# Self-attention with a distance decay in a decoder layer: the diagonal's triangles cleared on GpSimd, zero rows in the operands, two operand buffers, the memory turned during the first maxima

## The chip, the core and the metric

The kernel runs on one core of one Trainium2 chip. The metric is the device time of one execution in microseconds (us), taken as the median of the runs. The engines named here are TensorE (PE; its weight loads are PEld), VectorE (DVE), ScalarE (ACT), GpSimd (POOL) and SyncE (SP), which issues most DMAs.

## What is computed

One decoder layer on x of 1024 tokens by 128 features, in three residual steps, each on a layer norm of x:

```
x = x + self_attention(norm(x))        # 16 heads of 8 features, no causal mask
x = x + cross_attention(norm(x), ctx, mask)   # one head, 6404 memory rows
x = x + ffn(norm(x))                   # weights and activations rounded to FP4 blocks of 16
```

The change lies in the self-attention and in what prepares the cross-attention:

```
latent = (k + v) @ W_down_kv;  k_rec = latent @ W_up_k;  v_rec = latent @ W_up_v
scores = einsum(qh, k_rec) / sqrt(128)
scores = scores * exp(-0.01 * abs(t_q - t_k))
out    = softmax(scores) @ v_rec @ W_o
```

The factor exp(-0.01 |t_q - t_k|) splits into a product of a query part and a key part, but with other signs above the diagonal than below it. So there are two pairs of operands, QL and KL ("lower") and QU and KU ("upper"). Each is split into three bf16 parts that together carry nine products, hence 72 rows of 8 features; three further rows carry the negative row maximum of each query against ones in the keys.

## The kernel before

Heads are taken in four groups g of four heads. For each group and each half of the queries (eight half groups hg) the kernel does two things, one half group or so apart.

**Maxima.** For 16 units (4 heads x 4 tiles of 128 queries) PE multiplies QL by all 1024 keys KL (`max_unit`: two matmuls of 512 columns, 72 rows deep) into one of two pairs of PSUM banks, and DVE multiplies by the decay table and takes the row maximum (`max_unit` on DVE, line 671). After 16 units PE turns the maxima (`max_rows`, line 930), DVE splits them in three bf16 parts (`shift_split`) and SP stores them into row 72 to 74 of the query operands (`load_shift`, line 304, six DMAs).

**Scores, exponentials, values.** 64 blocks gb of four units: a unit is one head, one tile of 128 keys and 512 queries. PE writes its transposed scores into one of three banks (`scores`), ACT takes the exponential into `probs` (line 537), PE multiplies with the values into bank 3 (`pv`, line 969, float32, four heads side by side in 32 columns each). Units 0 and 2 of each block hold the diagonal: their 128x128 diagonal tile is neither wholly lower nor wholly upper. PE computes it from QL and KL without the maximum (72 rows), DVE multiplies it in PSUM by `diagT` (line 747), and PE adds the negative maximum with a matmul of `ones_rows` (line 958). ACT waits for that.

PE's order is written out by hand: the token list `ORDER` in each block, with two maxima turns ("A" and "B") between scores. DVE's order follows it: diagonal product, one maxima turn, twice in a block. So the scores of a block wait for DVE's queue. Maxima run `MAX_LEAD` = 9 turns ahead of a half group.

Operands live in three buffers (`NB = 3`), so groups 0 to 2 are loaded early. Ctx (3.28 MB, called mem) is loaded when the scores of group 1 are done, turned on PE in blocks 53 to 59 (`mem_tiles`, line 981) and split into high and low parts on DVE (`mem_parts`, lines 692 and 694) once the maxima are over. The FFN weights' scales are DVE work in blocks 8 to 10 (`weight_scales`). When the self-attention's last values are done, SP begins to load the mask pieces (512 KB each, line 352) of the cross-attention into the room of `v_ext`; only the first piece is there before. GpSimd turns each piece into floats (line 430), DVE adds it to the logits (line 775).

Of the kernel before, what the change touches and what calls it, by code (L numbers as in the profile page):

```python
# [23 lines left out]
SHIFT_ROW = 72  # L24
MATH_ROWS = 72
# [5 lines left out]
def decoder_layer(nc, x, ctx, mask, w_q, w_k, w_v, w_o, w_down_kv, w_up_k, w_up_v,  # L31
# [27 lines left out]
    MAX_LEAD = 9  # L59
    MEM_BLOCK = (NG * NH * UNITS - UNITS - MAX_LEAD + 3) // 2  # L60
    EARLY_BLOCK = NG * NH * (S // P) - 3
    SCALE_BLOCK = NT
# [4 lines left out]
    with ExitStack() as stack:  # L67
# [8 lines left out]
        SLOTS = 2 * PARTS - 1  # L76

# [3 lines left out]

        ident = sb("ident", [P, P])
        wq_sb = sb("wq_sb", [P, D]); wk_sb = sb("wk_sb", [P, D]); wv_sb = sb("wv_sb", [P, D])
        wo_sb = sb("wo_sb", [P, D]); wdn_sb = sb("wdn_sb", [P, DL])
        wuk_sb = sb("wuk_sb", [DL, D]); wuv_sb = sb("wuv_sb", [DL, D])
        xw_sb = sb("xw_sb", [P, D]); xwT = sb("xwT", [P, D]); xb_sb = sb("xb_sb", [P, 1])
        half_neg = sb("half_neg", [P, NT])
        ones_rows = sb("ones_rows", [P, P], BF16)
# [11 lines left out]
        diagT = sb("diagT", [P, P])  # L100
# [6 lines left out]

        memT_lo = sb("memT_lo", [P, NK * P], F32R)
        qc = sb("qc", [P, 2, P])
# [5 lines left out]
        NB = 3  # L115
        OPW = HG * S
        with ExitStack() as self_stack:
            def sb1(name, shape, dt=F32):
                return self_stack.enter_context(nc.sbuf_tensor(name, shape, dt))
            ops = [sb1(f"operands_{b}", [P, 4, HG, S], BF16) for b in range(NB)]  # L120
            probs = sb1("probs", [P, 2 * HG, BANK])
# [8 lines left out]
        memT_hi = sb("memT_hi", [P, NK * P], F32R)  # L130
        fb = sb("fb", [P, 4, FF]); sb("pad_2", [P, OPB - NK * D - 4 * FF])
        logits_1 = sb("logits_1", [P, S2]); sb("pad_3", [P, 16 * BANK - S2])
# [20 lines left out]
        def early_turn(k):  # L153
            return (None, 1, 2, 4, 5, 6)[k] if 0 <= k < 6 else -1
# [18 lines left out]
        ones_src = xqT[:, 0:P // 2].bitcast(BF16)  # L173
        xT = ops[2][:, 2, 0:2, :].rearrange("p h n -> p (h n)").bitcast(F32)
# [7 lines left out]
        parts_sb = ops[1][:, 0:PARTS, :, :].rearrange("p w h n -> p (w h) n").rearrange("p (w a) n -> p w a n", w=4)  # L182
        iota_i = ops[2][:, 0, 0:4, :].rearrange("p h n -> p (h n)")[:, 0:2 * (2 * S - P)].bitcast(I32)
        iota_d = ops[2][:, 1, 0:4, :].rearrange("p h n -> p (h n)")[:, 0:2 * (2 * S - P)].bitcast(I32)
# [3 lines left out]
        s_tab = sem("tables_ready"); s_one = [sem(f"ones_loaded_{b}") for b in range(NB)]; s_pool = sem("pool_chain"); s_ones = sem("ones_rows_ready")  # L188
# [13 lines left out]
        s_dr = sem("diag_scores_ready"); s_dd = sem("diag_decayed")  # L202
        s_st = sem("scoresT_ready"); s_sd = sem("diag_scoresT_ready"); s_p = sem("probs_ready"); s_pv = sem("pv_block_done"); s_ot = sem("oT_taken")
# [3 lines left out]
        s_ql = sem("qc_low_ready"); s_mlo = sem("memT_low_ready"); s_mhi = sem("memT_high_ready"); s_dg = sem("diagT_ready")  # L207
# [43 lines left out]
        ROW_BANKS = (4, 5, 7)  # L251

# [8 lines left out]
        def _(sp):  # L261
# [18 lines left out]
            def load_ones(b):  # L280
                for w in (KL, KU):
                    sp.dma_start(ops[b][SHIFT_ROW:FULL_ROWS, w, :, :].rearrange("p h (a n) -> p (h a) n", n=P),
                                 ones_src[0:PARTS, :].unsqueeze(1).broadcast_to([PARTS, HG * S // P, P])).then_inc(s_one[b], 16)

            def load_operand(g, w):

# [10 lines left out]

            def load_shift(hg):
# [8 lines left out]
            sp.wait_ge(s_ones, 1)  # L307
            load_ones(0)
# [9 lines left out]
            load_ones(1)  # L318
            for w in range(4):
                load_operand(1, w)  # L320
            load_shift(1)
            sp.wait_ge(s_iota2, 1)
            sp.wait_ge(s_tab, 2)
            sp.wait_ge(s_v, 1)
            load_ones(2)
            for w in range(4):
                load_operand(2, w)
            load_shift(2)
            sp.wait_ge(s_st, 1 * 2 * BLKS)
            for w in range(4):  # L330
                load_operand(3, w)
            load_shift(3)
            load_shift(4)
            sp.wait_ge(s_st, 2 * 2 * BLKS)
            sp.dma_start(mem[:, 0:NKF, :], ctx[0, 0:NKF * P].rearrange("(t p) d -> p t d", p=P)).then_inc(s_mem, 16)
            sp.dma_start(mem[0:KREM, NKF, :], ctx[0, NKF * P:S2]).then_inc(s_mem, 16)
            for hg in range(5, NG * NH):
                load_shift(hg)
            sp.wait_ge(s_mxd, NG * NH * UNITS)
            sp.dma_start(mask_room(0, MP), mask[0, 0:P, 0:MP]).then_inc(s_mk0, 16)  # L340

            for t in range(NT + 1):
                for m in range(NMP if t < NT else 0):
# [3 lines left out]
                    if n == 1:  # L347
                        sp.wait_ge(s_pv, NG * BLKS)
# [12 lines left out]
        def _(pool):  # L361
            chain = [0]

            def link(ins):
# [12 lines left out]
            link(pool.memset(ones_src[:, :], 1.0))  # L377
            pool.affine_select(out=ones_rows[:, :], in_=ones_src[:, :], compare_op=ALU.is_ge, fill=0.0, base=-SHIFT_ROW,
                               pattern=[[0, P]], channel_multiplier=1).then_inc(s_ones, 1)
            pool.wait_ge(s_ones, 1)  # L380
# [9 lines left out]
            pool.wait_ge(s_iota2, 1)  # L390
            pool.wait_ge(s_dg, 1)
# [30 lines left out]

            def mask_piece(n):
# [10 lines left out]
            for n in range(NMP + 1 + LEAD // 2):  # L434
                if n == 1:
                    rstd_of(0, s_o6, s_o7)
# [18 lines left out]
        def _(act):  # L455
# [6 lines left out]

            act.wait_ge(s_wk, 16 * 5)
# [39 lines left out]
            act.wait_ge(s_mt, 1)  # L503
            act.activation(diagT[:, :], PS[:, 5, 0:P], ACT.Copy).then_inc(s_dg, 1)

            def take_oT(half):
                act.wait_ge(s_pv, NT * (half + 1))
# [21 lines left out]
            for g in range(NG):  # L529
                for b in range(BLKS):  # L530
                    gb = g * BLKS + b
                    for h in range(HG):
                        u = gb * HG + h
                        act.wait_ge(s_st if h % 2 else s_sd, 2 * gb + h // 2 + 1)
                        if gb >= 2 and h == 0:
                            act.wait_ge(s_pv, gb - 1)
                        act.activation(probs[:, (gb % 2) * HG + h, :], PS[:, u % 3, :], ACT.Exp).then_inc(s_p, 1)  # L537
                        if h % 2 == 1:
                            attn_step(0, early_turn(2 * (gb - EARLY_BLOCK) + h // 2))

                    if gb > 0 and gb % NT == 0:
                        take_oT(gb // NT - 1)
# [69 lines left out]
        def _(dve):  # L612
# [10 lines left out]

            dve.wait_ge(s_x, 16)
# [61 lines left out]
            def mem_parts(c):  # L686
                k0, kw = chunk(c)
                src = PS[:, 4 + c % 4, 0:kw]
                dve.wait_ge(s_mt, c + 2)
                if c == 0:  # L690
                    dve.wait_ge(s_st, 3 * 2 * BLKS)
# [174 lines left out]
        def _(pe):  # L866
# [186 lines left out]
            for gb in range(NG * BLKS):  # L1053
                u, mu = gb * HG, UNITS + MAX_LEAD + 2 * gb
                c = 2 * (gb - MEM_BLOCK)
                for tok in ORDER:
                    if tok == "s0": shift_diag(u)
# [145 lines left out]
```

## Time and profile before

| what | value |
|---|---|
| median of 3 runs (lowest to highest) | 581.99 us (580.92 to 586.65) |
| the profiled execution | 584.69 us, span 583.0 us, mean granted clock 0.893 |
| PE busy | 504.6 us, 87% |
| DVE busy | 403.5 us, 69% |
| ACT busy | 301.2 us, 52% |
| POOL busy | 102.3 us, 18% |
| chain of waits by engine | PE 66%, DVE 25%, issue 3%, DMA 2% |

Three stages share the span: preparation and first maxima to 65.6 us, the 64 blocks to 292.0 us, the cross-attention and FFN after that. The granted clock is the share of TensorE's full 2.4 GHz that was granted; 0.50 is 1.2 GHz. A busy share is an average over these stages, so it does not tell which engine holds up which stage.

### The profile page before, as it was taken

The page shows a single profiled execution, that of the slowest core. Times are in us where ns is not written, and L with a number is a line of the kernel's source. Part 1 is how long each engine was busy: PE and PEld are TensorE (multiplying, and loading weights), DVE is VectorE, ACT ScalarE, POOL GpSimd, SP SyncE. Part 2 cuts the span into 40 slices and gives each one's busy share as a digit, 9 for nine tenths or more (in the row PEclk, how much of TensorE's full clock was granted, in tenths as well). Part 3 has the DMA queues.
Part 4 walks back from the last instruction along what each step waited for, and adds up shares of the span by engine and source line. Part 5 has one row for each costly group of instructions (what it writes and reads, how often), then busy time and mean ns, then how long its engine had stood idle before and what let it go on. Part 6 is the DMA issues. An engine that isn't in the chain of part 4 may idle for free.

```text
span 583.0 us, 9028 instructions
## 1 busy us (share of the span) xinstructions
PE 504.6 (87%) x3222; PEld 321.0 (55%) x3222; DVE 403.5 (69%) x1026; ACT 301.2 (52%) x601; POOL 102.3 (18%) x119
## 2 busy tenths in 40 slices
PE   7258999889999999999887998989899898989953
PEld 6101233223233333345365997978789797878851
DVE  3889869879698988889377345756646566664443
ACT  4710256447475757677716572726446372638420
POOL 6020000980000000000034322221312212210000
PEclk9755579879698989899989998989989998999985
DMA  2690535307000800001057524323232422400000
GB/s 65 191 276 22 102 66 103 65 2 161 5 1 3 226 3 1 3 3 37 1 190 224 146 83 117 115 72 110 87 110 86 146 87 79 139 15 6 1 6 5
DMA packets 20727, 46.04 MB, mean 79 GB/s; under 512 B 4470, under 2 KB 9786, under 8 KB 20106
## 3 DMA queue, kind: packets, MB, share of 16 engines
q1 hardware_dynamic: 19930, 44.74, 27.9%
q8 instruction: 26, 0.43, 0.3%
q0 software_dynamic: 224, 0.54, 0.3%
q10 hardware_dynamic: 528, 0.18, 0.2%
q14 instruction: 19, 0.16, 0.1%
HBM read 40.39 MB, written 4.72 MB: 77 GB/s over the span
## 4 chain that ended last, share of the span: by engine, by line
PE 66%; DVE 25%; issue 3%; DMA 2%; ACT 2%; POOL 0%; SPq 0%; DVEq 0%; ACTq 0%; POOLq 0%
PE banks L868 43%; PE banks L969 11%; DVE banks L671 8%; PE banks L1101 6%; PE banks L958 3%; DVE logits L775 3%; DVE fa L811 1%; DMA operands<-query_parts 1%; DVE qc_lo L729 1%; PE banks L981 1%; DVE fa L810 1%; DVE fa L806 1%; DVE f_small L802 1%; ACT probs L537 1%; DMA x_sb<-in_x 1%
## 5 line engine op out<-in xcount | busy, mean ns | idle before, releaser
L537 ACT ACTIVATE probs<-banks 128x512 f32<-128x512 f32 x256 | 139.1, 596 | 117.4 <-PE banks L958 115.3
L868 PE MATMUL banks<-operands 72*128 72x512 bf16 (+5 forms) x704 | 158.3, 360 | 14.6 <-DMA operands<-query_parts 8.0
L671 DVE CUSTOM_DVE_ANT_0 banks<-banks,decay 128x1024 f32<-128x1024 f32 x128 | 156.5, 1228 | 15.1 <-PE banks L868 11.2
L868 PEld LDWEIGHTS banks<-mem,pT 128*128 128x128 f32 (+1 forms) x816 | 107.9, 195 | 7.7
L868 PE MATMUL banks<-mem,pT 128*128 128x128 f32 (+1 forms) x816 | 111.5, 279 | 0.0
L868 PEld LDWEIGHTS banks<-operands 72*128 72x128 bf16 (+1 forms) x704 | 62.0, 104 | 82.1 <-DVE row_max L671 24.5
L775 DVE CUSTOM_DVE_ANT_0 logits<-banks,mring 128x512 f32<-128x512 f32 (+1 forms) x102 | 67.4, 668 | 46.6 <-PE banks L868 23.2
L559 ACT ACTIVATE pT<-banks 128x512 f32<-128x512 f32 (+1 forms) x104 | 60.4, 581 | 52.6 <-PE banks L1101 52.6
L969 PE MATMUL banks<-probs,v_ext 128*32 128x512 f32 x512 | 76.6, 673 | 0.7 <-ACT probs L537 0.7
L430 POOL TENSOR_SCALAR mring<-mring 128x1024 f32<-128x1024 int32 (+1 forms) x55 | 52.7, 959 | 90.3 <-DMA mring<-in_mask_BxSxS_ik 88.1
L868 PE MATMUL banks<-memT_hi,qc_hi 128*128 128x512 f32 (+1 forms) x104 | 50.4, 485 | 17.7 <-DVE cmax L775 17.7
L1101 PE MATMUL banks<-ident,logits 128*128 128x128 f32 (+1 forms) x408 | 63.5, 279 | 0.0
L549 ACT ACTIVATE logits<-logits,neg_max 128x1024 f32<-128x1024 f32 (+1 forms) x56 | 58.8, 1051 | 6.4 <-DVE neg_max L782 6.4
L958 PEld LDWEIGHTS banks<-operands,ones_rows 75*128 75x128 bf16 x128 | 12.5, 98 | 83.8 <-DVE banks L747 67.9
L747 DVE TENSOR_TENSOR banks<-banks,diagT 128x128 f32<-128x128 f32 x128 | 40.6, 317 | 21.1 <-PE banks L868 21.0
L1101 PEld LDWEIGHTS banks<-ident,logits 128*128 128x128 f32 (+1 forms) x408 | 49.4, 143 | 4.0 <-issue 2.0
L868 PE MATMUL banks<-memT_hi,qc_lo 128*128 128x512 f32 (+1 forms) x104 | 41.4, 398 | 0.0
L868 PE MATMUL banks<-memT_lo,qc_hi 128*128 128x512 f32 (+1 forms) x104 | 41.1, 395 | 0.0
L958 PE MATMUL banks<-operands,ones_rows 75*128 75x128 bf16 x128 | 29.8, 233 | 12.5 <-DVE banks L747 12.3
L420 POOL TENSOR_TENSOR rstd<-mv,half_neg 128x1 f32<-128x1 f32 x16 | 8.8, 552 | 146.3 <-DVE mv L817 83.2
L868 PEld LDWEIGHTS banks<-memT_hi,qc_hi 128*128 128x128 f32 x104 | 20.7, 199 | 20.4 <-DVE cmax L775 19.7
L430 POOL TENSOR_SCALAR mask<-mask 128x1024 f32<-128x1024 int32 x1 | 1.0, 1046 | 135.5 <-DMA mask<-in_mask_BxSxS_ik 135.5
(162 smaller groups left out, 456.0 us busy)
## 6 DMA issues: line engine op xcount, KB each, us to landing
mring<-in_mask_BxSxS_ik SPq DMA_DIRECT2D x47, 512.0 KB, 3.5
operands<-key_parts SPq DMA_DIRECT2D x24, 192.0 KB
operands<-query_parts SPq DMA_DIRECT2D x24, 192.0 KB
key_parts<-operands SPq DMA_DIRECT2D x10, 256.0 KB, 3.5
query_parts<-operands SPq DMA_DIRECT2D x4, 384.0 KB, 4.7
mring<-in_mask_BxSxS_ik SPq DMA_DIRECT2D x8, 130.0 KB, 2.1
operands<-shift_parts SPq DMA_DIRECT2D x48, 4.0 KB, 1.7
x_sb<-in_x SPq DMA_DIRECT2D x1, 512.0 KB, 4.4
```

What stands on the lines that cost most here:

```text
L420: pool.tensor_tensor(rstd[:, t:t + 1], mv[:, t, 1:2], half_neg[:, t:t + 1], ALU.pow).then_inc(done, 1)
L430: pool.tensor_scalar(src.bitcast(F32), src, -1.0, -NEG, ALU.add, ALU.mult).then_inc(s_ma, 1)
L537: act.activation(probs[:, (gb % 2) * HG + h, :], PS[:, u % 3, :], ACT.Exp).then_inc(s_p, 1)
L549: act.activation(y, y, ACT.Exp, bias=neg_max[:, t:t + 1], accum_out=esum[:, t, e:e + 1]).then_inc(s_e, 1)
L559: last = act.activation(pT[:, n % 3, 0:o], PS[:, 2 + n % 2, 0:o], ACT.Copy)
L671: dve.tensor_tensor_reduce(out=rows, in0=rows, in1=decay[:, off:off + S], scale=1.0, scalar=-3.0e38, op0=ALU.mult, op1=ALU.max, accum_out= ...
L747: dve.tensor_tensor(PS[:, u % 3, c0:c0 + P], PS[:, u % 3, c0:c0 + P], diagT[:, :], ALU.mult).then_inc(s_dd, 1)
L775: dve.tensor_tensor_reduce(out=logits_sb(t)[:, k0:k0 + kw], in0=PS[:, logits_bank(n), 0:kw], in1=mk, scale=1.0, scalar=-3.0e38, op0=ALU.ad ...
L868: return pe.matmul(o, a, b, start=start, stop=stop)
L958: pe.matmul(PS[:, u % 3, d0:d0 + P], ones_rows[0:FULL_ROWS, :], queries(gb // BLKS % NB, QL, half)[0:FULL_ROWS, h, d0:d0 + P], start=False ...
L969: last = pe.matmul(PS[h * VW:(h + 1) * VW, 3, :], v_ext[:, kt, g * HG + h, :], probs[:, (gb % 2) * HG + i, :], start=(b % NT == 0), stop=( ...
L1101: last = pe.transpose(PS[0:kw, 2 + n % 2, j * P:(j + 1) * P], logits_sb(t)[:, k * P:k * P + kw], ident[:, :])
```

## The change

1. A block's diagonal units take their diagonal tile as if it were lower (with the maximum's rows). For every pair of blocks there is a ninth unit with the four heads' diagonal tiles computed as upper. ACT takes all nine exponentials; GpSimd then clears one triangle in each of the four lower tiles and the other triangle in the ninth unit (`affine_select`), and PE adds the ninth unit's values in `pv_diag`. `diagT`, `ones_rows`, the DVE product and the adding matmul are gone.
2. Forty rows of zeros stand between the 72 rows of parts and the three rows of the maximum, which move to row 112: maxima are 112 rows deep and scores 115 rows. The zeros come by DMA from a zeroed piece of `oT`, once for each buffer.
3. Two operand buffers instead of three. The decay table, the parts and the iotas lie elsewhere; the parts lie where the turned memory will be.
4. mem is loaded right behind the first group's lower operands, turned on PE in maxima turns 8 to 20 into banks 0 to 3, copied to its high part on ACT, reduced to its low part by a matmul with the negative identity on PE, and copied again on ACT. It lies in the room of operand buffer 1, so that buffer's constants and operands are loaded after it is turned, and mem is loaded a second time when the last scores are done.
5. `MAX_LEAD` is 7. The weights' scales stand ahead of the first maximum on DVE. `rstd` of tile 0 moves into the pairs on GpSimd.

```diff
-SHIFT_ROW = 72
-MATH_ROWS = 72
+PART_ROWS = 72
+MATH_ROWS = 112
+SHIFT_ROW = 112
...
-        NB = 3
+        NB = 2
...
+            def load_constants(b):
+                for w in range(4):
+                    sp.dma_start(ops[b][PART_ROWS:MATH_ROWS, w, :, :],
+                                 zero_rows.unsqueeze(1).broadcast_to([MATH_ROWS - PART_ROWS, HG, S])).then_inc(s_one[b], 16)
...
             load_operand(0, KL)
             load_operand(0, QL)
+            load_mem()
             store_parts(QU)
             store_parts(KU)
             load_operand(0, QU)
             load_operand(0, KU)
+            sp.wait_ge(s_mt, NC)
+            load_constants(1)
+            load_operand(1, KL)
+            load_operand(1, QL)
             load_shift(0)
...
             sp.wait_ge(s_mxd, NG * NH * UNITS)
             sp.dma_start(mask_room(0, MP), mask[0, 0:P, 0:MP]).then_inc(s_mk0, 16)
+            sp.wait_ge(s_st, PAIRS * PU)
+            load_mem()
...
+            for n in range(PAIRS):
+                d0 = 2 * n % NT // 2 * P
+                for j in (0, 2, 4, 6):
+                    diag = probs[:, j, d0:d0 + P]
+                    pool.wait_ge(s_p, n * PU + j + 1)
+                    pool.affine_select(out=diag, in_=diag, compare_op=ALU.is_ge, fill=0.0, base=0,
+                                       pattern=[[1, P]], channel_multiplier=-1).then_inc(s_sel, 1)
+                pool.wait_ge(s_p, (n + 1) * PU)
+                upper = probs[:, 2 * HG + n % 2, :].rearrange("p (h q) -> p h q", h=HG)
+                pool.affine_select(out=upper, in_=upper, compare_op=ALU.is_ge, fill=0.0, base=-1,
+                                   pattern=[[0, HG], [-1, P]], channel_multiplier=1).then_inc(s_sel, 1)
...
+            def mem_high(c):
+                act.wait_ge(s_mt, c + 1)
+                if c == 0:
+                    for w in range(4):
+                        act.wait_ge(s_scr[w], 16 * (SLOTS if w in (KL, KU) else NH))
+                act.activation(memT_hi[:, k0:k0 + kw], PS[:, c % 4, 0:kw], ACT.Copy).then_inc(s_mhi, 1)
...
+            def mem_rest(c):
+                pe.wait_ge(s_mhi, c + 1)
+                pe.matmul(PS[:, c % 4, 0:kw], ident_n, memT_hi[:, k0:k0 + kw], start=False, stop=True,
+                          skip_group_check=True).then_inc(s_mls, 1)
...
+            pe.wait_ge(s_mlo, NC)
+            for n in range(PAIRS):
+                mu, k = UNITS + MAX_LEAD + 4 * n, 4 * (n - EARLY_PAIR)
+                scores(n, 0)
+                max_turn(mu)
+                scores(n, 1)
+                if n > 0:
+                    pv(2 * n - 1)
+                scores(n, 2)
+                max_turn(mu + 1)
+                early(k)
+                scores(n, 3)
+                if n > 0:
+                    pv_diag(n - 1)
+                scores(n, 4)
+                max_turn(mu + 2)
+                early(k + 1)
+                scores(n, 5)
+                scores(n, 6)
+                pv(2 * n)
+                scores(n, 7)
+                max_turn(mu + 3)
+                early(k + 2)
+                scores(n, 8)
+                early(k + 3)
```

The order of SP's first loads before, from the stores of the lower parts on (a row is a DMA, with how often it is repeated):

```order
L277 DMA query_parts<-operands 128x3x512 x2
L296 DMA operands<-key_parts 24x4096 x3
L296 DMA operands<-query_parts 24x2x2048 x3
L277 DMA query_parts<-operands 128x3x512 x2
L272 DMA key_parts<-operands 128x1024 x5
L296 DMA operands<-query_parts 24x2x2048 x3
L296 DMA operands<-key_parts 24x4096 x3
L304 DMA operands<-shift_parts 1x16x128 x6
```

and in the changed kernel (oT holds the zeros and the ones):

```order
L280 DMA query_parts<-operand_parts 128x3x512 x2
L301 DMA operands<-key_parts 24x4096 x3
L301 DMA operands<-query_parts 24x2x2048 x3
L304 DMA mem<-in_ctx 128x50x128
L305 DMA mem<-in_ctx 4x128
L280 DMA query_parts<-operand_parts 128x3x512 x2
L275 DMA key_parts<-operand_parts 128x1024 x5
L301 DMA operands<-query_parts 24x2x2048 x3
L301 DMA operands<-key_parts 24x4096 x3
L285 DMA operands<-oT 40x4x1024 x4
L288 DMA operands<-oT 3x4x1024 x2
L301 DMA operands<-key_parts 24x4096 x3
L301 DMA operands<-query_parts 24x2x2048 x3
L313 DMA operands<-shift_parts 1x16x128 x6
```

The shift rows of half group 0, without which no scores begin, moved behind the load of mem, the constants of buffer 1 and the lower operands of group 1; the second of them waits for all of mem's tiles to be turned.

PE in one block before, a block with two maxima units:

```order
L958 MATMUL banks<-operands,ones_rows 128x128
L868 MATMUL banks<-operands 128x512
L868 MATMUL banks<-operands 128x256
L868 MATMUL banks<-operands 128x128 x2
L868 MATMUL banks<-operands 128x512 x3
```

and about one pair of blocks in the changed kernel, from one diagonal unit (128x128 x4) to the next:

```order
L880 MATMUL banks<-operands 128x128 x4
L880 MATMUL banks<-operands 128x512 x4
L984 MATMUL banks<-probs,v_ext 32x512 x4
L880 MATMUL banks<-operands 128x512 x4
L995 MATMUL banks<-probs,v_ext 32x128 x4
L880 MATMUL banks<-operands 128x512 x5
L984 MATMUL banks<-probs,v_ext 32x512 x4
L880 MATMUL banks<-operands 128x512 x3
L880 MATMUL banks<-operands 128x128 x4
```

The single matmuls of 128 columns that waited for DVE are gone; four diagonal tiles and a quarter-width product with the values came in their place.

## Rows read from the trace of the kernel before

**Rows 1.** Windows: each engine's busy us (instructions), granted clock, DMA share, GB/s

```profile
core 0: us, PE busy (x) PEld busy (x) DVE busy (x) ACT busy (x) POOL busy (x), PEclk, DMA share, GB/s
40.00:50.00 10.00, 8.59 (x18) 1.05 (x16) 10.00 (x17) 0.00 (x0) 0.00 (x0) 0.50 0.44 97
65.60:80.20 14.60, 14.21 (x56) 4.92 (x55) 9.12 (x18) 6.49 (x12) 0.00 (x0) 0.52 0.72 137
80.20:292.00 211.80, 197.31 (x1307) 76.19 (x1305) 176.99 (x391) 136.06 (x256) 28.10 (x29) 0.93 0.18 42
```

**Rows 2.** Timeline of PE: start, us, operation, [idle before <-releaser]; maxima and scores begin

```profile
33.44 1.86 PE L868 MATMUL banks<-operands 72*128 72x512 bf16 x4 [7.96 <-DMA operands<-query_parts]
...
65.64 0.29 PE L958 MATMUL banks<-operands,ones_rows 75*128 75x128 bf16 x1
```

**Rows 3.** Timeline of PE, one block at full clock

```profile
162.57 1.06 PE L969 MATMUL banks<-probs,v_ext 128*32 128x512 f32 x8
163.57 0.23 PE L958 MATMUL banks<-operands,ones_rows 75*128 75x128 bf16 x1
...
165.56 1.06 PE L969 MATMUL banks<-probs,v_ext 128*32 128x512 f32 x8
```

**Rows 4.** Timeline of PE where one half group's maxima end

```profile
177.88 0.23 PE L958 MATMUL banks<-operands,ones_rows 75*128 75x128 bf16 x1 [1.36 <-DVE banks L747]
...
179.58 1.94 PE L969 MATMUL banks<-probs,v_ext 128*32 128x512 f32 x8
```

**Rows 5.** Timeline of DVE: last parts, first maximum, one weight's scales, diagonal product

```profile
30.87 1.29 DVE L664 TENSOR_TENSOR operands<-probs,operands 128x512 bf16<-128x512 f32 x2
34.63 1.23 DVE L671 CUSTOM_DVE_ANT_0 banks<-banks,decay 128x1024 f32<-128x1024 f32 x1 [2.47 <-PE banks L868]
...
99.60 0.55 DVE L680 TENSOR_REDUCE turnT<-wg_raw 128x24 f32<-128x384 f32 x1
...
100.82 0.29 DVE L747 TENSOR_TENSOR banks<-banks,diagT 128x128 f32<-128x128 f32 x1
```

**Rows 6.** Timeline of PE where mem is turned

```profile
265.90 0.60 PE L981 MATMUL banks<-ident,mem 128*128 128x128 f32 x4
266.34 0.38 PE L868 MATMUL banks<-operands 75*128 75x512 bf16 x1
```

**Rows 7.** Timeline of ACT, four exponentials in a row

```profile
280.77 2.22 ACT L537 ACTIVATE probs<-banks 128x512 f32<-128x512 f32 x4 [0.51 <-PE banks L958]
```

**Rows 8.** Timeline of SP's queue: start, us to issue, DMAs

```profile
26.16 1.14 SPq L296 DMA_DIRECT2D operands<-query_parts  x3
...
30.07 2.70 SPq L272 DMA_DIRECT2D key_parts<-operands  x5
...
56.32 3.78 SPq L304 DMA_DIRECT2D operands<-shift_parts  x6
...
188.15 0.85 SPq L335 DMA_DIRECT2D mem<-in_ctx  x1
189.04 9.36 SPq L336 DMA_DIRECT2D mem<-in_ctx  x1
```

**Rows 9.** Windows as in Rows 1: loading a group's four operands, loading mem

```profile
61.80:79.40 17.60, 16.85 (x59) 5.19 (x58) 12.30 (x24) 5.69 (x11) 0.00 (x0) 0.50 0.71 136
190.00:200.00 10.00, 10.00 (x78) 3.95 (x71) 9.67 (x21) 7.26 (x15) 0.00 (x0) 1.00 1.03 290
```

**Rows 10.** Timeline of POOL: a select of 128x128, a slow operation of 128x384

```profile
1.07 0.29 POOL L370 TENSOR_SCALAR_AFFINE_SELECT ident<-ident 128x128 f32<-128x128 f32 x1
...
104.45 1.50 POOL L410 TENSOR_SCALAR wdT<-wdT 128x384 f32<-128x384 f32 x1
```

**Rows 11.** Timelines of PE, SP, POOL and DVE where the cross-attention begins

```profile
290.98 1.07 PE L969 MATMUL banks<-probs,v_ext 128*32 128x512 f32 x8 [0.73 <-ACT probs L537]
292.11 36.70 SPq L352 DMA_DIRECT2D mring<-in_mask_BxSxS_ik  x16
295.89 1.05 POOL L430 TENSOR_SCALAR mring<-mring 128x1024 f32<-128x1024 int32 x1 [8.58 <-DMA mring<-in_mask_BxSxS_ik]
298.20 0.69 DVE L775 CUSTOM_DVE_ANT_0 logits<-banks,mring 128x512 f32<-128x512 f32 x1
```

More of the change, by code:

```diff
@@ L526, in attn_step @@
                     act.activation(qc_hi[:, t % 2, :], qc[:, t % 2, :], ACT.Copy).then_inc(s_q2, 1)
[L529 to L542, printed above, removed]
+            for n in range(PAIRS):
+                for j in range(PU):
+                    u = n * PU + j
+                    act.wait_ge(s_st, u + 1)
+                    if j == 2 * HG and n >= 2:
+                        act.wait_ge(s_pu, n - 1)
+                    if j % HG == 0 and j < 2 * HG and n >= 1:
+                        act.wait_ge(s_pv, 2 * n + j // HG - 1)
+                    to = j if j < 2 * HG else 2 * HG + n % 2
+                    act.activation(probs[:, to, :], PS[:, u % 3, :], ACT.Exp).then_inc(s_p, 1)
+                    if j == 3 and n > 0 and n % (NT // 2) == 0:
+                        take_oT(n // (NT // 2) - 1)
+                    if j in EARLY_AFTER:
+                        attn_step(0, early_turn(4 * (n - EARLY_PAIR) + EARLY_AFTER.index(j)))
             take_oT(NG * NH - 1)
@@ new lines, in side @@
+                def side(kq, h, kt, cols, **more):
+                    qs, ks = (QL, KL) if kq == "lower" else (QU, KU)
+                    return mm(bank[:, cols] if kq != "diag" else bank[:, h * P:(h + 1) * P],
+                              operand(g % NB, ks)[0:FULL_ROWS, h, kt * P:(kt + 1) * P],
+                              queries(g % NB, qs, half)[0:FULL_ROWS, h, cols], **more)
+                if j == 2 * HG:
+                    kt = half * TPB + b % NT // 2
+                    d0 = kt % TPB * P
+                    for h in range(HG):
+                        last = side("diag", h, kt, slice(d0, d0 + P), start=(h == 0), alone=True)
+                elif j % 2 == 1:
+                    h, kt, _ = unit(b, j % HG)
+                    last = side("lower" if kt < half * TPB else "upper", h, kt, slice(0, BANK))
+                else:
+                    h, kt, _ = unit(b, j % HG)
+                    d0 = kt % TPB * P
+                    last = side("lower", h, kt, slice(d0, BANK))
+                    if d0 > 0:
+                        last = side("upper", h, kt, slice(0, d0), start=False, alone=True)
@@ new lines, in _ @@
+                step = mu - MEM_UNIT
+                if 0 <= step < NC:
+                    mem_tiles(step)
+                if MEM_LAG <= step < NC + MEM_LAG:
+                    mem_rest(step - MEM_LAG)
+            pe.wait_ge(s_mlo, NC)
+            for n in range(PAIRS):
+                mu, k = UNITS + MAX_LEAD + 4 * n, 4 * (n - EARLY_PAIR)
[21 more added lines that the diff above has]
+                early(k + 3)
```

277 lines of the change are left out of this document (112 added, 165 removed).

## The prediction, made before the changed kernel was run

> **What bounds the kernel now.** I read the windows first, since the page's shares are averages over stages. Of the 583.0 us span, the first 65.6 us are preparation and first maxima, 226.4 us the 64 blocks of scores, and the rest does not change but for its start. In the blocks PE is busy nearly throughout, 14.2 of 14.6 us and 197 of 212 us [rows 1], so matmuls set their pace. But 14.6 us stand at a granted clock of 0.52, and the rest at 0.93. A block at full clock lasts 2.99 us from one product with the values to the next (162.57 to 165.56), 1.00 us of it that product; the other 1.99 us hold 4,352 columns (four maxima and four score units' worth of 512, two times 128 for the shifts), 0.234 us for 512 [rows 3]. 64 such blocks would be 191 us: 35 us go into the lower clock and into waits. The waits are those for DVE's diagonal product: at 177.88 us PE has sat idle for 1.36 us, and the product that follows takes 1.94 us instead of 1.06 [rows 4]. The pattern returns where DVE splits a half group's maxima; it is what part 1 of the change can win.
>
> In the first stage DVE sets the pace: lower operands land at 33.44 us, the first maximum starts at 34.63 us and takes 1.23 us, and the first shift matmul stands at 65.64 us [rows 2, 5].
>
> **The change, part by part.** First the pairs. A pair has 8,192 columns of maxima and full units and 512 of the ninth unit, 3.98 us at the rate above, two products with the values (2.0 us), and a quarter-width one, some 0.25 us: 6.2 us against 5.98 now. So a pair costs 0.2 us more at full clock; the gain is in what no longer happens. ACT has nine exponentials of 0.555 us [rows 7], 5.0 us: hidden while PE needs 6.2. DVE keeps four maxima, 4.9 us, hidden. GpSimd has four selects of 0.29 us [rows 10] and one of 512 wide; that one is not in the trace, so 0.6 us (four times the elements at 128x128's fixed part) to 2.0 us (the slow 128x384 operation scaled by 4/3) [rows 10]. Sum 1.8 to 3.2 us of 6.2, and each select has one or two units of PE work between its exponential and its reader: hidden. Maxima fill 27 of the 32 pairs (108 turns from turn 23 on); the last five are ACT-bound at about 5.2 us. At seven half-group borders PE turns the maxima right after the turn before and must wait for DVE's 1.23 us; with the turning itself, 1.0 us each. Tail after the last score: exponential, select, last product, 2 us. I add 3 us for a start at the low clock (half the 6 us or so that I suppose it lasts; the bound above is the 14.6 us of rows 1, worth 7, the bound below 0). Sum: 27 x 6.2 + 5 x 5.2 + 7 + 2 + 3 = 205 us, for 226.4 now: **21 us saved**.
>
> Then the start. DVE now does three weights' scales ahead of the first maximum: 3 x 1.22 us (99.60 to 100.82) from 32.16 us, so the first maximum starts at 35.8 us instead of 34.6 [rows 5]. Behind the lower query operands (issued until 27.3) SP issues mem [rows 8]. Its 3.28 MB take 11.3 us at 290 GB/s [rows 9], behind operands that land at 33.4: mem is there at about 45, when the eighth maximum is due (35.8 + 7 x 1.23 = 44.4). No loss there. But the second DMA of mem held SP's queue for 9.36 us when the first was in flight [rows 8], so SP is free again only at about 42, not 28.2, and the stores of the upper parts (2.1 MB, 7 us at the same rate) end at about 52; now they are issued by 32.8 (30.07 + 2.70 [rows 8]). ACT's first `mem_high` waits for just these stores, since the high part lies where the parts lie; PE's first `mem_rest`, in turn 10, waits for ACT, and turn 11's maxima stand behind it. PE passes turn 10 at 53.4 us, DVE idle for some 4 us.
>
> Each further turn has maxima (0.47 us), four transposes (0.44, from 265.90 to 266.34 [rows 6]) and the subtracting matmul (0.23): 1.14 us at full clock, beside DVE's 1.23 and ACT's two copies of 0.56; tightly chained I take 1.4, and twice the PE time, 2.3, for the first two after the idle stretch. The last tiles are turned in turn 20: 53.4 + 2 x 2.3 + 8 x 1.4 + 1.2 (split of the maxima) = 70 us.
>
> Only then may SP go on, and the shift rows of half group 0 stand behind 1.31 MB of zeros and 1.18 MB of lower operands in the same queue. The loads of group 1 now move 2.36 MB in 17.6 us, 136 GB/s, though the share is only 0.71, while mem runs at 1.03 and 290 GB/s [rows 9]: few-row transfers are slow. The zero rows have the same shape of packets, so I price both at 136: 18.3 us. Wake-up and first issue add 1.5: the shift rows land at 90 us, against 60 (56.32 + 3.78 [rows 8]) and a use at 65.6 [rows 2]. Bound below: the queue's data hold nothing up and only SP's issue counts (18 DMAs, 9 us), at 78 us; above: mem's turns all at the low clock, at 99 us. **The scores start 24 us later.**
>
> The Trainium skill, DMA: Bandwidth & Descriptors, section Why a DMA increments its semaphore by 16 and not by 1, says that a DMA is spread over the largest count up to 16 that divides its slowest dimension: 12 engines for 24 rows, 10 for 40. The 0.71 agrees with 12 of 16; by that rule the zeros would take 12/10 of my price, and the scores start at 92 us, not 90.
>
> Last, the cross-attention. mem is issued when the last scores are done, 2 us before the end of the last product. It holds SP for 0.85 + 9.36 us [rows 8], to 8.3 us behind that end; the second mask piece (the first of the ring) is issued then and lands 3.8 us later (292.11 to 295.89), at 12.1, against 3.9 now. DVE's third mask addition stood at 6.2 us behind the end (298.20 against 292.0), 1.3 us of it not owed to the mask's landing and its 1.05 us on GpSimd [rows 11]: it starts at 13.3, **7 us later**, and what follows is a chain. Bounds 3 (mem's rows issued early enough, with DVE catching up) and 10 (low clock after the wait). The second mem itself is needed some 30 us later: hidden. HBM traffic grows by 3.3 MB, hidden else.
>
> Sum: 24.4 - 21.4 + 7.5 = +10.5, taken as +11: span 594, profiled time 596, and by the median, which lies 2.7 us below the profiled 584.69, **593 us**.
>
> **The rivals.**
>
> *Faster.* The same mechanisms, but the start is cheap: packets of the zeros run like mem's, shift rows don't wait behind earlier data, so the scores start at 78; zero rows or steadier PE work keep the clock up from the first pair, and borders cost nothing: 200 us. 78 + 200 = 278, 14 less than 292, with 5 for the masks: 573 us. For it: no row shows a queue's earlier data holding back a later small DMA. Against it: the three waits are in the program's order, and each has a row. It decides where the scores start before about 84 us with a phase of 203. 0.15.
>
> *No change.* Part of that: scores at 84, phase of 203, masks 5 us late: 582 - 5 + 5, 582 us. 0.2.
>
> *Slower still.* The low clock lasts: in the first maxima PE was busy 86% at a granted 0.50 with 72-row operands (40 to 50 us) and its clock did not rise, and 0.52 stands for the first 14.6 us of the scores too [rows 1]. Should the deeper operands not alter that, mem's turns add 8 us and the first pairs 4: 605 us. 0.12.
>
> *The change does not do what it says.* GpSimd or ACT takes DVE's place as what PE waits for: ACT's nine exponentials with the copy of `oT` would have to take over 6.2 us a pair, or a wide select over 3 us. Then a pair is 7 us, 20 us more: 613. Nothing speaks for it but shared access of DVE and GpSimd. 0.05.
>
> The forecast has 0.48.
>
> **How the numbers follow.** What this measurement can tell from no change is about 1%, 5.8 us. Faster takes the first rival, 0.15. Within 1% takes the second: 0.2. Slower: the forecast, and both slower rivals, 0.65. The range: start 78 to 99, phase 197 to 212, masks 3 to 10 give 568 to 612 if all fall on one side; leaving out a tenth on each side, 574 to 607.
>
> **What would show it.** No diagonal product on DVE and PE's waits for it gone; clock near 1.00 from the second or third pair to the end; pairs of 6.2 us. PE's `mem_rest` with a first wait of 2 to 4 us on ACT, ACT's on a DMA. An SP queue in which mem's second DMA takes 9 us twice. Shift rows landing near 90 us with PE idle for over 10 us. After the last block PE and DVE waiting 7 us on the masks. I am wrong if the scores start before 84 us (then the queue's order costs less than its bytes), or if a pair takes under 6 us.

## The result and the profile after

The changed kernel takes **598.88 us** (median of four runs, 598.05 to 600.09) against 583.01 us for the kernel before on the same chip (four runs, 580.92 to 586.65): a ratio of **1.027, interval 1.021 to 1.032**, so slower, and inside the predicted range (574 to 607, forecast 593). Single executions of the kernel before spread widely (575 to 594 us over all chips used here, the longer ones at a lower granted clock), so each ratio is taken from its faster runs alone and is not the quotient of the two medians. The profiled run took 599.18 us with a span of 597.1 at a granted clock of 0.916; before, the span was 583.0.

The page's first part and its chain of waits (shares of the span by engine and by line) for the kernel after:

```profile
PE 497.0 (83%) x3394; PEld 320.6 (54%) x3394; DVE 363.7 (61%) x874; ACT 334.4 (56%) x659; POOL 157.9 (26%) x277
...
PE 65%; DVE 15%; SPq 8%; DMA 5%; issue 3%; ACT 2%; POOL 1%; DVEq 0%; ACTq 0%; POOLq 0%
PE banks L880 45%; PE banks L984 10%; PE banks L1127 6%; SPq L305 4%; DVE banks L706 3%; DVE logits L787 2%; PE banks L995 2%; DMA mring<-in_mask_BxSxS_ik 2%; DVE fa L823 1%; ACT probs L571 1%; DMA operands<-shift_parts 1%; SPq L285 1%; SPq
```

DVE did lose work (403.5 us before, 363.7 now, and 15% of the chain for 25%). What is new in the chain is SP's queue, at 8%: L305 is the second DMA of mem, L285 the zero rows. The queue's timeline (start, us to issue, DMAs), which answers to [rows 8] and [rows 11], shows where:

```profile
25.99 1.13 SPq L301 DMA_DIRECT2D operands<-query_parts  x3
27.48 0.86 SPq L304 DMA_DIRECT2D mem<-in_ctx  x1
28.38 13.05 SPq L305 DMA_DIRECT2D mem<-in_ctx  x1
41.48 2.05 SPq L280 DMA_DIRECT2D query_parts<-operand_parts  x2
...
64.68 5.44 SPq L285 DMA_DIRECT2D operands<-oT  x4
70.16 4.64 SPq L288 DMA_DIRECT2D operands<-oT  x2
74.84 3.10 SPq L301 DMA_DIRECT2D operands<-key_parts  x3
77.99 1.19 SPq L301 DMA_DIRECT2D operands<-query_parts  x3
79.22 3.77 SPq L313 DMA_DIRECT2D operands<-shift_parts  x6
...
292.14 0.80 SPq L304 DMA_DIRECT2D mem<-in_ctx  x1
292.99 9.54 SPq L305 DMA_DIRECT2D mem<-in_ctx  x1
302.58 2.59 SPq L358 DMA_DIRECT2D mring<-in_mask_BxSxS_ik  x4
```

On PE's side, the first memory low part, one turn of the turning, the first scores (compare [rows 2]), and a pair from the middle (compare [rows 3]):

```profile
50.79 0.51 PE L1013 MATMUL banks<-memT_hi,qc_hi 128*128 128x512 f32 x1 [0.97 <-ACT memT_hi L524]
...
52.26 0.61 PE L880 MATMUL banks<-operands 112*128 112x512 bf16 x2
...
53.38 0.61 PE L880 MATMUL banks<-operands 112*128 112x512 bf16 x2
...
88.03 5.71 PE L880 MATMUL banks<-operands 115*128 115x512 bf16 x13 [21.27 <-DMA operands<-shift_parts]
...
152.54 1.06 PE L984 MATMUL banks<-probs,v_ext 128*32 128x512 f32 x8
153.54 1.92 PE L880 MATMUL banks<-operands 115*128 115x512 bf16 x12
155.38 1.06 PE L984 MATMUL banks<-probs,v_ext 128*32 128x512 f32 x8
156.38 1.04 PE L880 MATMUL banks<-operands 115*128 115x256 bf16 x5
```

A turn is 1.12 us here (52.26 to 53.38), and the scores begin 22.4 us later than before, after 21.27 us of idle PE: PE waited for the shift rows, which stand behind four other rows of the queue. Windows (columns as in [rows 1]) put the clock beside that:

```profile
88.00:94.30 6.30, 6.27 (x21) 1.91 (x21) 3.87 (x6) 3.73 (x7) 0.88 (x3) 0.55 0.48 109
94.30:294.00 199.70, 194.87 (x1460) 67.43 (x1454) 136.86 (x240) 158.42 (x293) 56.31 (x159) 1.00 0.12 29
```

After some 6 us the granted clock goes to full and stays there to the end of the phase, where [rows 1] had 0.52 for 14.6 us and 0.93 after. Last, POOL and DVE where the cross-attention begins (compare [rows 11]):

```profile
308.49 1.04 POOL L445 TENSOR_SCALAR mring<-mring 128x1024 f32<-128x1024 int32 x1 [13.71 <-DMA mring<-in_mask_BxSxS_ik]
...
309.57 0.69 DVE L787 CUSTOM_DVE_ANT_0 logits<-banks,mring 128x512 f32<-128x512 f32 x1 [9.25 <-POOL mring L445]
```

So the span splits into three differences. The scores start at 88.03 instead of 65.64: +22.4. The phase lasts 206.1 us (to 294.1) instead of 226.4: -20.3. From its end to the end of the span it is 303.0 us instead of 291.0: +12.0. Together +14.1, the difference of the spans.

### The profile page after: what moved, and what is told of

Its sections match the earlier page's. It is cut to its first block, busy times and chain, and to the rows that moved or that the text cites. A ratio compares the mean times of both kernels' runs of the same rounds, so it can differ in the third digit from the quotient of the medians.

```text
span 597.1 us, 9530 instructions
## 1 busy us (share of the span) xinstructions
PE 497.0 (83%) x3394; PEld 320.6 (54%) x3394; DVE 363.7 (61%) x874; ACT 334.4 (56%) x659; POOL 157.9 (26%) x277
## 4 chain that ended last, share of the span: by engine, by line
PE 65%; DVE 15%; SPq 8%; DMA 5%; issue 3%; ACT 2%; POOL 1%; DVEq 0%; ACTq 0%; POOLq 0%
PE banks L880 45%; PE banks L984 10%; PE banks L1127 6%; SPq L305 4%; DVE banks L706 3%; DVE logits L787 2%; PE banks L995 2%; DMA mring<-in_mask_BxSxS_ik 2%; DVE fa L823 1%; ACT probs L571 1%; DMA operands<-shift_parts 1%; SPq L285 1%; SPq L301 1%; DMA xb_sb<-in_L_xattn_b 1%; SPq L288 1%
## 5 line engine op out<-in xcount | busy, mean ns | idle before, releaser
L571 ACT ACTIVATE probs<-banks 128x512 f32<-128x512 f32 x288 | 159.0, 600 | 63.6 <-PE banks L880 58.0
L880 PE MATMUL banks<-operands 112*128 112x512 bf16 (+4 forms) x736 | 150.3, 337 | 46.1 <-DMA operands<-shift_parts 21.3
L880 PEld LDWEIGHTS banks<-operands 115*128 115x128 bf16 (+1 forms) x736 | 55.9, 99 | 153.3 <-ACT probs L571 57.8
L880 PEld LDWEIGHTS banks<-mem,pT 128*128 128x128 f32 (+1 forms) x816 | 109.4, 197 | 8.0
L880 PE MATMUL banks<-mem,pT 128*128 128x128 f32 (+1 forms) x816 | 113.0, 282 | 0.0
L428 POOL TENSOR_SCALAR_AFFINE_SELECT probs<-probs 128x128 f32<-128x128 f32 x128 | 37.5, 293 | 133.5 <-ACT probs L571 133.4
L984 PE MATMUL banks<-probs,v_ext 128*32 128x512 f32 x512 | 68.2, 605 | 0.7 <-ACT probs L571 0.5
L432 POOL TENSOR_SCALAR_AFFINE_SELECT probs<-probs 128x512 f32<-128x512 f32 x32 | 20.3, 634 | 41.3 <-ACT probs L571 41.3
L612 ACT ACTIVATE xqT<-banks 128x128 f32<-128x128 f32 x8 | 2.2, 277 | 38.3 <-PE banks L1164 38.3
L880 PEld LDWEIGHTS banks<-memT_hi,qc_lo 128*128 128x128 f32 x104 | 20.4, 196 | 4.5
```

The costliest lines, as they stand in the source:

```text
L428: pool.affine_select(out=diag, in_=diag, compare_op=ALU.is_ge, fill=0.0, base=0, pattern=[[1, P]], channel_multiplier=-1).then_inc(s_sel, 1)
L432: pool.affine_select(out=upper, in_=upper, compare_op=ALU.is_ge, fill=0.0, base=-1, pattern=[[0, HG], [-1, P]], channel_multiplier=1).then ...
L571: act.activation(probs[:, to, :], PS[:, u % 3, :], ACT.Exp).then_inc(s_p, 1)
L880: return pe.matmul(o, a, b, start=start, stop=stop, skip_group_check=alone)
L984: last = pe.matmul(PS[h * VW:(h + 1) * VW, 3, :], v_ext[:, kt, g * HG + h, :], probs[:, (gb % 2) * HG + i, :], start=(b % NT == 0), stop=( ...
```

## The experiments

Ratios are to the kernel before, run on the same chip; the median of all its runs was 585.5 us beside experiments one to four, 581.3 beside five, six, seven and nine, 581.6 beside eight and ten, 583.0 above. The changed kernel is the base unless another is named.

**One: mem's second load on ScalarE's queue.**

```diff
-            sp.wait_ge(s_st, PAIRS * PU)
-            load_mem()
 # on ScalarE, behind its last copy of oT:
+            act.dma_start(mem[0:KREM, NKF, :], ctx[0, NKF * P:S2]).then_inc(s_mem, 16)
+            act.dma_start(mem[:, 0:NKF, :], ctx[0, 0:NKF * P].rearrange(...)).then_inc(s_mem, 16)
```

> The changed kernel with mem's second load issued from ACT's queue behind the last copy of oT, its small part first, so that SP's queue is free for the mask pieces at once. Queue theory: the third mask addition on DVE stood 15.5 us behind the last product with the values and goes back to about 7 (6.2 before the change, and some sharing of bandwidth); 8 to 12 us less than the change, about 588 to 590 us. Rival (the bytes of mem hold the masks back, not the queue): both transfers share the DMA engines, the piece lands only 2 to 3 us earlier than in the change, about 596 us.

Measured 590.38 us (590.11 to 593.17): 8.5 us less than the changed kernel, as the queue theory had it. SP issues masks at once when the phase ends (293.7), and DVE goes on 6.2 us after it, as before the change:

```profile
293.79 16.07 SPq L356 DMA_DIRECT2D mring<-in_mask_BxSxS_ik  x8
...
299.88 0.69 DVE L787 CUSTOM_DVE_ANT_0 logits<-banks,mring 128x512 f32<-128x512 f32 x1
```

The same bytes move, but in another order: the first of these mask pieces is now issued at 293.79, ahead of mem's large part (294.52), where in the changed kernel it stands behind it, 8.5 us after the phase's end. So the order of the issues cost the time, and not that these bytes have to be moved. The edit changes mem's queue and the order of its two parts together; no run tells them apart.

**Two: the shift rows ahead of group 1's constants and operands.**

```diff
+            load_shift(0)
             sp.wait_ge(s_mt, NC)
             load_constants(1)
             load_operand(1, KL)
             load_operand(1, QL)
-            load_shift(0)
```

> The changed kernel with the shift rows of half group 0 issued ahead of SP's wait for mem's turned tiles. Queue theory: PE starts the scores at about 67 us instead of 88, the blocks' stage keeps its 206 us but for a new wait of 3 to 6 us at group 1's first maxima, whose operands still come behind the constants: 598.9 - 21 + 5 = 583 us. Rival (the start is bound by bytes, so the wait only moves): PE then waits at group 1's first maxima for most of the 21 us, 595 us or more.

Measured 583.35 us (581.86 to 585.27), 15.5 us less. The queue and PE:

```profile
62.68 3.80 SPq L313 DMA_DIRECT2D operands<-shift_parts  x6
66.52 5.41 SPq L285 DMA_DIRECT2D operands<-oT  x4
...
68.66 3.38 PE L880 MATMUL banks<-operands 115*128 115x512 bf16 x13 [0.48 <-ACT memT_lo L529]
...
87.71 1.44 PE L880 MATMUL banks<-operands 112*128 112x512 bf16 x3 [5.14 <-issue]
```

The scores start at 68.66, right behind mem's last turn: 19.4 us earlier. But group 1's maxima then wait 5.14 us (the profile names no releaser; by experiments five and six it is the loads of group 1), and the clock is low from 87.1 to 94.0, so 15.5 of the 19.4 us arrive at the end.

**Three: no zero rows** (operands 75 deep as before the change).

```diff
-MATH_ROWS = 112
-SHIFT_ROW = 112
+MATH_ROWS = 72
+SHIFT_ROW = 72
-                for w in range(4):
-                    sp.dma_start(ops[b][PART_ROWS:MATH_ROWS, w, :, :], zero_rows...).then_inc(s_one[b], 16)
```

> The changed kernel without the forty zero rows: maxima 72 and scores 75 rows deep as before, nothing else altered. If the clock stays up because no matmul waits for DVE any more, the blocks' stage keeps its 206 us and its granted clock of 1.00, and the scores start some 6 to 8 us earlier, since four DMAs that took 5.4 us to issue are gone: about 591 us. Rival (the deeper rows hold the clock): the clock falls at borders as in the kernel before, the first pairs stay at the low clock for 10 us or more, the stage takes 215 us or more: 600 us or more.

Measured 594.55 us (592.67 to 596.6), 4.3 us less, and between the theory (591) and the rival (600 or more). The scores start 7.8 us earlier, at 80.23, but the phase is longer:

```profile
80.20:94.20 14.00, 13.96 (x46) 4.06 (x46) 6.45 (x10) 6.56 (x12) 2.05 (x6) 0.52 0.24 49
94.20:290.00 195.80, 190.97 (x1432) 66.08 (x1431) 134.37 (x236) 155.69 (x288) 55.26 (x156) 1.00 0.13 29
```

At 0.52 the first 14.0 us run as slowly as they did before the change, as the rival had it, and then the clock holds at 1.00 without a zero row, as the theory had it. So the new kernel holds the clock without the zero rows. They shorten the low stretch at the start (to some 6 us), but the scores start 7.8 us later with them.

**Four: both queue edits.**

> Both queue edits together (mem's second load on ACT's queue, shift rows of half group 0 first). Queue theory: they touch different stages and add up, about 598.9 - 16 - 10 = 573 us, faster than the kernel before by 1.5%. Rival: if each gives little by itself, 590 us or more.

Measured 576.56 us (575.01 to 578.27, ten runs), ratio 0.997, interval 0.993 to 1.001: 22.3 us less than the changed kernel, where one and two alone give 24.0. The wait for group 1 stands as in two (5.71 us at 86.92), with the low clock from 84.6 to 91.5, and the time stays 3.6 us above the 573 expected.

**Five: four, without zero rows, and group 1's operands ahead of its ones.**

```diff
             sp.wait_ge(s_mt, NC)
-            load_constants(1)
             load_operand(1, KL)
             load_operand(1, QL)
+            load_constants(1)
```

> The memory's second load on ScalarE's queue, the shift rows ahead of group 1, no zero rows, and group 1's first keys and queries ahead of its ones. Theory (the costs are transfers in SyncE's order, and they add): 576.6 less 4.3 (what dropping the zero rows gave alone) less 5.7 (TensorE's wait for group 1's operands at 86.9) = 566 to 570. Rival (without the zero rows the clock stays low longer at the start of the scores, or another transfer stands in the same place): 573 to 577.

Measured **569.05 us** (566.58 to 574.96), ratio **0.985, interval 0.979 to 0.990**: the fastest of all. The phase in a window:

```profile
68.10:271.90 203.80, 198.83 (x1476) 68.70 (x1477) 141.49 (x248) 162.07 (x299) 57.66 (x162) 1.00 0.18 39
```

No wait of PE over 0.51 us is left in it, and the clock is 1.00 throughout.

**Six: as five, but with the zero rows kept.**

> As the version with both queue edits (576.6), with group 1's first keys and queries issued ahead of its zero and one rows; the zero rows stay. Theory: the 5.7 us wait of TensorE at 86.9 and the low clock behind it (85.1 to 92.0) go: 570 to 572. Rival (the wait is for buffer 1 as a whole, so the constants that now come last hold the same maxima up): 575 to 578.

Measured 576.14 us (573.97 to 577.35), no gain on four: the rival is right. The wait only moved from the operands to the zeros and ones, which now come last:

```profile
70.43 5.09 SPq L285 DMA_DIRECT2D operands<-oT  x4
75.56 3.67 SPq L288 DMA_DIRECT2D operands<-oT  x2
...
88.37 0.94 PE L880 MATMUL banks<-operands 112*128 112x512 bf16 x3 [4.54 <-DMA operands<-oT]
```

Against five, zero rows cost 7.1 us here.

**Seven: five, with the stores of the upper parts ahead of mem's first load.**

```diff
-            load_mem()
             store_parts(QU)
             store_parts(KU)
+            load_mem()
```

> As the version of both queue edits without zero rows, and the stores of the upper queries and keys issued ahead of the memory's first load, which now lies behind them. Theory (the start of the scores waits for the turned memory, not for the upper parts): the memory comes some 2 us later, 0 to 3 us slower than that version. Rival (the upper operands and the shift rows behind them set it): 3 to 8 us faster, since the memory's second transfer held SyncE for 13.05 us ahead of these stores.

Measured 571.77 us (570.34 to 572.75), 2.7 us more than five, as the theory had it: PE now waits 6.00 us for mem at 51.92, and the start moves with it. The stores behind mem were not what set the start.

**Eight: the selects left out.** GpSimd counts them off without doing them, so the upper part of the diagonal blocks isn't cleared.

> The changed kernel with GpSimd's five selects of each pair left out (GpSimd still counts each of them off in its place), so the upper part of the diagonal blocks isn't cleared. Theory (GpSimd's 158 us of work lie beside TensorE's): the time stays at 597 to 600. Rival (TensorE waits for selects, or they slow VectorE's reads): a pair shorter than 6.37 us by at least 0.15, so 5 us or more faster, 594 or less.

Measured 599.2 us (598.64 to 599.73), 0.3 from the changed kernel. The selects are hidden whole.

**Nine: the kernel before with the zero rows,** in all three buffers, and nothing else.

```diff
-SHIFT_ROW = 72
-MATH_ROWS = 72
+PART_ROWS = 72
+SHIFT_ROW = 112
+MATH_ROWS = 112
...
+                for w in range(4):
+                    sp.dma_start(ops[b][PART_ROWS:MATH_ROWS, w, :, :]..., ones_rows[0:MATH_ROWS - PART_ROWS, :]...)
```

> The kernel before with the operands 115 rows deep: 40 zero rows in each of its three buffers, nothing else changed. Theory A (the order of the new phase, without a wait on VectorE in the pairs, keeps the clock at 1.00): the low stretches between 110 and 302 stay, and the time is that of before within 2 us. Theory B (the deeper rows keep the clock up, whatever the order): the 31 us of low clock between 110.9 and 237.2 mostly go, and it is 5 to 15 us faster than before.

Measured 576.12 us (574.84 to 578.33), ratio 0.995, interval 0.992 to 0.999, in spite of a new wait of 6.19 us for group 1's constants at 86.12. The first of these windows is the kernel before, from 160 us:

```profile
160.00:210.00 50.00, 47.28 (x315) 17.85 (x308) 44.14 (x99) 32.40 (x61) 0.00 (x0) 0.93 0.25 68
```

and this is the same stretch with zero rows, with one of its waits for DVE's diagonal product:

```profile
160.00:210.00 50.00, 47.18 (x332) 18.30 (x334) 46.53 (x102) 34.93 (x66) 0.00 (x0) 1.00 0.24 68
...
173.86 0.23 PE L963 MATMUL banks<-operands,ones_rows 115*128 115x128 bf16 x1 [1.36 <-DVE banks L751]
```

PE is busy for as long (47.2 us) and waits the same 1.36 us for the same product, but the clock stays at 1.00 instead of 0.93. It stays there from 90.2 us to the end of the phase, and at the start of the scores it rises after 7.1 us, where before it took 14.0:

```profile
90.60:284.00 193.40, 178.80 (x1268) 71.03 (x1267) 170.24 (x378) 132.59 (x250) 28.14 (x29) 1.00 0.25 53
```

In the trace theory B is right: the deeper rows hold the clock even in the old order. In time the gain is small, 5.2 us by the medians and 2.8 by the ratio, for the "5 to 15" expected; the new wait takes 6.2 us back. The rows may also lie behind the kernel before's spread: its runs beside these took 575.3 us at a granted clock of 0.910 to 590.7 at 0.883, and those of this version lie within 3.5 us.

**Ten: as nine, but the maxima 72 rows deep, and groups 1 and 2 load operands ahead of zeros and ones.**

> The kernel before with the 40 zero rows, but the maxima 72 rows deep as before, so that only scores read the zero rows and ones, and groups 1 and 2 load operands ahead of their zeros and ones. Against 576.1 for zero rows everywhere. Theory A (the depth of the score matmuls is enough to hold the clock): the low stretches behind 110 stay away, and TensorE's 6.2 us wait at 86 with its low clock of 83.7 to 90.6 goes too: 566 to 571. Theory B (the maxima, more than half of the columns, need the depth): the low stretches come back, and the time is within 3 us of the kernel before's, 578 to 584.

Measured 573.07 us (571.25 to 574.24), ratio 0.988, interval 0.984 to 0.992: nearer to theory A, though 2 us outside its range. The wait at 86 is gone, and from 122.1 us the clock holds:

```profile
122.70:279.80 157.10, 148.93 (x1067) 60.01 (x1066) 137.06 (x305) 111.14 (x210) 6.11 (x8) 1.00 0.16 41
```

Before that, it fell twice (108.5 to 111.9 and 118.7 to 122.1), which it did not do there in nine. So the depth of the scores does most; that the maxima's does the rest is likely and not shown, since the order of the loads changed with it.

## Why the prediction was right, and where its terms were off

**The start.** First maximum at 35.8 predicted, 36.22 measured. mem's second DMA holding SP until about 42: 41.4. The first memory low part passed at 53.4: 50.79, since the stores behind mem took less. PE's wait for ACT there was 0.97 us, for "2 to 4". The turns: 1.4 us each and two of 2.3 predicted, the first six 1.12 measured, since the granted clock was 1.00 from 49.4 on, while mem was being turned; so the tiles were turned at 64.6, not at 70. Then the error went the other way. From the first constant's issue to the first scores it took 23.4 us, not 19.8. The bytes were not all of it. SP alone spent 14.5 us (64.68 to 79.22) to issue the 12 DMAs ahead of the shift rows, 10.1 us of them for six DMAs of constants, and the rows landed 5.0 us after their last issue. The two errors, 5.4 and 3.6 us, partly cancel, and that is luck: scores at 88.0 for 90. The other price that the Trainium skill gave (DMA: Bandwidth & Descriptors, section Why a DMA increments its semaphore by 16 and not by 1), 2 us more for the zeros, points to the side on which the measured interval lies, but the windows over the zeros (share 0.45 and 0.36) don't show which part is engines and which is issue; it is neither borne out nor refuted. Experiment two shows the step itself: with the shift rows ahead, the start is at 68.7. Experiment seven bears out that mem, and not the stores behind it, sets that earlier start.

**The phase.** 205 predicted, 206.1 measured, and the parts hold: pairs of 6.37 us (2.85 + 3.52 between products with the values) for 6.2, a border pair of 7.16 for 7.2, late pairs of 5.29 for 5.2, low clock of some 6 us for "6 us or so". The 0.17 us more in a pair are 4.6 us over the 27; the quarter-width product took 0.36 us (157.35 to 157.71), for 0.25. The other terms were put too high by nearly as much, the borders among them (0.8 us for 1.0), so the 1.1 us is closer than its terms. POOL and ACT are hidden, as said (experiment eight; the wide select took 634 ns, near the low bound of 0.6 to 2.0 us).

What I could only name together, "35 us into the lower clock and into waits", can be taken apart by windows over the phase: before, PE was idle for 14.9 us of it and the mean clock was 0.90, worth 22.6 us; after, 4.9 us and 0.99, worth 2 to 3:

```profile
65.60:292.00 226.40, 211.52 (x1361) 81.11 (x1360) 186.11 (x409) 142.54 (x267) 28.10 (x29) 0.90 0.22 49
...
88.00:294.10 206.10, 201.24 (x1476) 69.37 (x1476) 140.74 (x246) 162.15 (x299) 57.29 (x162) 0.99 0.13 31
```

Multiply a phase's length by its mean granted clock, and what remains is about its length at full clock (an estimate that treats waits as if they ran with the clock):

| kernel | phase, us | mean clock | product | less a wait for group 1 |
|---|---|---|---|---|
| before | 226.4 | 0.90 | 203.8 | 203.8 |
| changed | 206.1 | 0.99 | 204.0 | 204.0 |
| three, no zero rows | 209.8 | 0.97 | 203.1 | 203.1 |
| five | 203.8 | 1.00 | 203.8 | 203.8 |
| six | 210.0 | 0.99 | 207.9 | 203.4 |
| nine, before with zero rows | 218.0 | 0.97 | 211.5 | 205.3 |
| ten | 213.3 | 0.97 | 206.9 | 206.9 |

(Clock and length from windows over the phase; three from its two windows above. The clock has two digits, so a product is good to about 1 us. Nine's wait lay partly in the low clock, so its last figure may be 1.4 us too low.) The products before and after agree: what the new order saves in waits (10 us), the longer pair takes back (27 times 0.4 us against two blocks of 2.99), and by this estimate **the 20 us won are, on balance, the clock**. The others lie within about 3 us of them. Two things of this change hold the clock: the new order, without DVE in the score path (three and five), and the deeper operands (nine). After the low stretch at the start, either one does it alone. The waits for DVE's diagonal product, which I had put as the thing to be won, were real as idle time and went (10 of 14.9 us), but the added matmuls use them up; they are all still there in nine, which is faster than the kernel before.

**The cross-attention.** This is the step that was mis-sized: DVE's third mask addition, "7 us later" (7.5 in the sum), came 9.3 us later (15.5 behind the phase's end, for 6.2), and "what follows is a chain" hid another 2.7 us. The issue of the mask piece came as predicted, 8.5 us behind the phase's end (302.58) for 8.3. But the piece took 5.9 us to land on POOL's side (308.49) where it took 3.8 before [rows 11]: it now follows mem's 3.28 MB, whose bytes were still moving (DMA share 1.05, 302 to 304 us). That is 2.1 of the missing 2.3 us; issued ahead of mem, in experiment one, it took 3.85 again (293.79 to POOL at 297.64). Beside the other 2.7 us stands a low clock in PE's own wait and behind it: 10.2 us of it from 305.4, where before 3.4 us stood, and 3.4 us more from 322.4. That it makes up the 2.7 us is argued, not shown. In experiment one the mask addition comes 6.2 us after the end again, and the time drops by 8.5.

**The sum.** +24.4 - 21.4 + 7.5 = +10.5 predicted, +22.4 - 20.3 + 12.0 = +14.1 measured. The cross-attention is 4.5 us of the difference, the phase 1.1, the start -2.0. The rest of the 5.9 us between 593 and 598.88 is the step from the profiled run to the median: I took 2.7 us off, as for the kernel before, and the changed kernel's profiled run lay only 0.3 above its median.

**The rivals.** "Faster" needed the start before 84 and a cheap wait for masks; experiment four makes both true by hand and comes to 576.6, where that rival said 573. "No change" needed a start at 84: measured 88. "Low clock" did not come to pass: it lasted some 6 us of the scores, and most of mem was turned at full clock. The rows alone did not do the latter: without zero rows, in experiment three, the clock rose at 49.3 too, and in nine, with 112-row maxima but no turning beside them, it was 0.50 up to 73 us. GpSimd or ACT as the bound: no.

**Still open.** Why exactly the order without DVE holds the clock is not isolated: no run took the waits of the old order away without changing its matmuls. The products stand on one profiled run each, and the kernel before varies from run to run; the profiled one (584.69 us) was above its median.

## What to carry to other kernels

A reordering that wins where it was aimed can lose the same amount at both ends, through the order of one DMA queue: walk the queue at every point where a load is added, and ask which small, urgent transfer now stands behind it. Before pricing an engine's idle time, multiply each phase by its granted clock; if the products agree, the difference is, on balance, in the clock, and a cheaper cure may do. Here the small edit of experiment ten (0.988 of the kernel before) comes within the measurement of the whole change with its queue mended and without its zero rows (0.985).

## What the runs showed of the hardware

- In this kernel TensorE's granted clock depended on how many rows the matmuls use. With the same order, the same waits of 1.36 us and the same busy time, it was 0.93 at 75 rows and 1.00 at 115 (160 to 210 us). The columns were the same; only rows of zeros were added. The Trainium skill (TensorE: Matmul & The Clock Gate, section Part 1: The HAM clock gate) says that the clock follows how busy the engine has been recently. By busy time (47.3 and 47.2 of 50 us) these two stretches are alike, and their clocks are not. Depth was neither needed nor always enough: in five 75 rows held 1.00 over the whole phase, and in nine the 112-row maxima ran at 0.50 from 40 to 50 us, PE busy 8.59 of 10 us, exactly as 72-row ones had.
- At the start of the scores the clock rose after 14.0 us with 75-row scores (before) and 13.5 (three), and after 7.1 (nine), 7.9 (ten) and 5.7 us (the changed kernel) with 115-row scores.
- mem's second DMA, four rows of 512 bytes, holds SP's queue 13.05 us when it follows 3.28 MB at the start, and 9.54 at the end; on ScalarE's queue, with the small part first, the two take 0.49 and 0.84 us to issue, with no DMA behind them there that could have been held.
- The constants' DMAs were dear to issue. The four of zeros took 5.44 us and the two of ones behind them 4.64; without the zeros the two of ones took 1.57 (three), and three loads of 24 rows took 1.19 right behind. From narrower pieces the four of zeros took 8.46 us in nine, and 16.85 in ten, where operands are issued right ahead of them.
